# Routing of a mixture of experts in two steps, with the first five slots taken from the first six tiles

## The reference, cut to what matters

```python
x = x + cross_attention(layernorm(x), ctx)
x = x + self_attention(layernorm(x))
h = layernorm(x)                                   # (1024, 512)
logits = h @ gate_w.T + gate_b                     # (1024, 8)
topv, topi = top_k(logits, 2)
gate = softmax(logits where chosen, else -inf)     # two gates a row
out = x + sum over the 2 chosen experts e of gate[e] * (h @ expert_w[e] + expert_b[e])
```

## Time and profile before

| | |
|---|---|
| Time, median of 3 runs | 764.32 us (762.08 to 765.07) |
| Profiled execution | 759.4 us, span of the core 757.6 us |
| Granted TensorE clock, mean of the span | 0.99 |
| PE busy | 735.5 us, 97% |
| DVE, ACT, POOL busy | 554.2, 407.7, 350.3 us (73%, 54%, 46%) |
| DMA | 78.99 MB, mean 104 GB/s |

### The profile page before, as it was taken

The page is one execution under the profiler, slowest core; times in us unless marked ns, Lnnn a source line. Parts: engine busy times, 40 slices in busy tenths (PEclk is TensorE's granted clock), DMA queues, the critical chain, the costliest instruction groups (busy, mean ns, idle before and its releaser), DMA issues. The chain is left out here.

```text
span 757.6 us, 23202 instructions
## 1 busy us (share of the span) xinstructions
PE 735.5 (97%) x9488; PEld 644.7 (85%) x9489; DVE 554.2 (73%) x1293; ACT 407.7 (54%) x930; POOL 350.3 (46%) x364
## 2 busy tenths in 40 slices
PE   8999999999999999999999999999899999599997
PEld 7899989999899998999999999997677777578884
DVE  6768796967868768687696786877889998722236
ACT  5455666565566556655566555664566664033330
POOL 0664566456455644555545745541422221246630
PEclk9999999999999999999999999999999999789999
DMA  8410301221111011010110101141862229544538
GB/s 285 153 34 26 121 3 58 65 71 59 33 34 58 11 58 53 11 61 2 58 65 2 58 9 59 57 168 57 346 268 98 118 114 363 195 136 165 183 129 326
DMA packets 23317, 78.99 MB, mean 104 GB/s; under 512 B 3344, under 2 KB 4752, under 8 KB 20144
## 3 DMA queue, kind: packets, MB, share of 16 engines
q1 hardware_dynamic: 19536, 65.50, 24.0%
q0 software_dynamic: 3680, 12.06, 4.8%
HBM read 58.93 MB, written 18.61 MB: 102 GB/s over the span
## 5 line engine op out<-in xcount | busy, mean ns | idle before, releaser
L934 DVE TENSOR_TENSOR ctx_parts_lo<-craw,ctx_parts_hi 128x1032 fp32r<-128x1032 f32 (+1 forms) x56 | 66.5, 1188 | 3.6 <-ACT ctx_parts_hi L653 3.5
L1450 PE MATMUL bank<-ctx_parts_hi,wparts 128*128 128x258 f32 x224 | 67.2, 300 | 0.0
L1452 PE MATMUL bank<-ctx_parts_lo,wparts 128*128 128x258 f32 x224 | 63.5, 283 | 0.0
L1475 PE MATMUL bank<-wparts,ctx_parts_hi 128*128 128x256 f32 x224 | 63.3, 283 | 0.0
L1451 PE MATMUL bank<-ctx_parts_hi,wparts 128*128 128x258 f32 x224 | 63.2, 282 | 0.0
L1478 PE MATMUL bank<-wparts,ctx_parts_lo 128*128 128x256 f32 x224 | 63.1, 282 | 0.0
L1477 PE MATMUL bank<-wparts,ctx_parts_hi 128*128 128x256 f32 x224 | 62.9, 281 | 0.0
L684 ACT ACTIVATE v<-bank 128x512 f32<-128x512 f32 x56 | 33.3, 594 | 54.4 <-PE bank L1478 53.7
L496 POOL TENSOR_TENSOR k_trig<-kb_even,const 128x258 f32<-128x258 f32 (+1 forms) x42 | 49.0, 1167 | 28.8 <-ACT kb_even L674 28.1
L688 ACT ACTIVATE wraw<-wraw,nmax 128x257 f32<-128x257 f32 x96 | 47.8, 501 | 22.1 <-DVE nmax L1027 21.9
L1450 PE MATMUL bank<-ctx_parts_hi,w_sums_hi 128*128 128x258 f32 x168 | 52.7, 313 | 0.0
(11 more groups left out here) (418 smaller groups left out, 2588.4 us busy)
## 6 DMA issues: line engine op xcount, KB each, us to landing
craw<-ctx_t_dram SPq DMA_DIRECT2D x32, 516.0 KB, 4.3
expert_lo<-weights_dram SPq DMA_DIRECT2D x8, 1024.0 KB, 13.1
expert_hi_scratch<-wraw SPq DMA_DIRECT2D x16, 512.0 KB, 2.6
wparts<-expert_hi_scratch SPq DMA_DIRECT2D x8, 1024.0 KB, 9.1
wraw<-weights_dram SPq DMA_DIRECT2D x5, 1024.0 KB, 5.2
expert_lo<-ffn_out_scratch SPq DMA_DIRECT2D x16, 256.0 KB, 5.4
x<-x_dram SPq DMA_DIRECT2D x8, 256.0 KB, 4.4
late_weights_raw<-weights_dram SPq DMA_DIRECT2D x2, 1024.0 KB, 5.8
```

Source lines behind the costliest of these rows:

```text
L934: dve.tensor_tensor(dst[1], src, dst[0].bitcast(F32), ALU.subtract).then_inc(s_clo, 1)
L1450: pe.matmul(psum, whi_i[:, i, cols], hi[:, i, :], start=own and i == 0, stop=False, skip_group_check=not own)
L1452: last = pe.matmul(psum, whi_i[:, i, cols], lo[:, i, :], start=False, stop=i == 1, skip_group_check=not own)
L1475: pe.matmul(psum, hi[:, i, rows], whi_i[:, i, :], start=own and u == 0 and i == 0, stop=False, skip_group_check=True)
```

## The change

The routing is done in two steps.

- **First step.** `EARLY` grows from five tiles to six (tiles 0 to 5). `EK` = 12 is the number of their choices. Besides the ranks, PE counts the pairs of each expert in those six tiles (`early_count`). An expert's slots that are full from these six tiles alone can be known before tiles 6 and 7 are: DVE counts them (`full`), gives the first five of all such slots (`FIRST_SLOTS`) the numbers 0 to 4, and makes their table in one pass: `first_payload` holds 5 columns of row numbers and 5 of gates, `at_place` for the twelve early choices is made in two parts of six (`ONEHOT_PARTS`). PE multiplies it (12 blocks, 96 records) between the output projection of tile 7 and `x3_transposed(6)`. Then DVE writes `gather_row`, `scatter_row` and `slot_gate` of the five, and POOL issues the first four gathers.
- **POOL.** Both last `ffn_ln` (tiles 6 and 7) now stand behind these four gathers, and ahead of the gather of slot 4.
- **DVE.** The addition of tile 6's projection and the layer norm statistics of tile 6 move behind the first step; the early logits of tile 5 move ahead of it. Behind the statistics ten small instructions find the five slots' experts and correct ranks and counts for what the first five slots took.
- **PE.** The slots begin (transposes of slot 0) right behind the logits of tile 7. Then `late_ranks()`, the product of slots 0 and 1, and then `late_table()`: one table for the other 18 slots (`REST`), 16 blocks with 36 columns (row numbers and gates), 128 records. The transposes of the gates move from before the first product to between slots 3 and 4.
- **SP.** The loads of the last two experts (6 and 7) come ahead of the stores of `xn3` of tiles 6 and 7.
- Tensors move to other memory: the gathers' buffers into `craw`, `route_r` and `kept` into a new view at the place of `xn`.

The core of the diff:

```diff
-EARLY = TILES - 3
-ON_R = 10
-PAIRS = SLOTS + 1
+EARLY = TILES - 2
+FIRST_SLOTS = EARLY - 1
+REST = SLOTS - FIRST_SLOTS
+EK = 2 * EARLY
@@ gpsimd
-                ffn_ln(TILES - 2)
-                ffn_ln(TILES - 1)
...
                 pool.wait_ge(s_x3pad, 16)
-                pool.wait_ge(s_x3d, 16 * TILES)
+                pool.wait_ge(s_x3d, 16 * EARLY)
                 pool.wait_ge(s_rows, 1)
                 for i in range(AHEAD):
                     gather(i)
+                ffn_ln(TILES - 2)
+                ffn_ln(TILES - 1)
+                gather(AHEAD)
                 pool.wait_ge(s_rows, 2)
-                for i in range(SLOTS - LATE):
+                scatter(0)
+                scatter(1)
+                pool.wait_ge(s_x3d, 16 * TILES)
+                pool.wait_ge(s_rows, 3)
+                gather(FIRST_SLOTS)
+                pool.wait_ge(s_rows, 4)
+                for i in range(2, SLOTS - LATE):
@@ vector, behind place_in_tile(early_k)
+                dve.tensor_tensor(full_flags, early_count..., rc(R_TILE + 1, EARLY)..., ALU.is_ge)
+                dve.tensor_reduce(full, full_flags, AX.X, ALU.add)
                 dve.wait_ge(s_ohi, T + 2)
                 dve.tensor_tensor(otlo[:], ...)
-                ffn_ln_apply(T - 1)
+                (full_before, first_slot, picked, picked_sum, past_full, spot_open, spot, in_first: 8 instructions)
                 dve.wait_ge(s_sc, TILES)
-                for group in place_groups[:2]:
-                    place_onehots(*group)
+                for k0, k1 in ONEHOT_PARTS:
+                    dve.tensor_tensor(at_place[:, k0:k1, :], ...)
+                gates_of(0, EARLY, "")
+                (first_payload: 2 instructions)
                 dve.wait_ge(s_xpb, T + 1)
                 (x of tile 7 added in two halves)
+                dve.tensor_tensor(x[:, T - 1, :], b_cp, x[:, T - 1, :], ALU.add)
+                dve.wait_ge(s_table, 1)
+                (first_second, gather_row, scatter_row, slot_gate of the first five)
+                (statistics of tile 6, then of tile 7; ffn_ln_apply(T - 1); ten small instructions)
                 logits_evac(T - 1)
                 top(T - 1)
@@ tensor
-                pe.wait_ge(s_xo, T)
-                stay_awake(b_cp, 2)
+                pe.wait_ge(s_lg, T - 1)
+                stay_awake(b_x3, 2)
...
                     last.then_inc(s_cp, 1)
+                pe.wait_ge(s_payload, 1)
+                (first table)
                 x3_transposed(T - 1)
...
-                (late ranks, table of rows, table of gates)
+                pe.wait_ge(s_ewlo, HALVES)
+                slot_transposed(0, 0, 0)
+                late_ranks()
+                pe.wait_ge(s_lg, TILES)
+                pe.wait_ge(s_experts, 1)
+                pe.wait_ge(s_ehi, 16 * NE)
+                expert_step(0, 0, 0)
+                pe.wait_ge(s_xo, T + 2)
+                expert_step(1, 1, 0)
+                late_table()
+                for i in range(2, FIRST_SLOTS - 1):
+                    expert_step(i, i, 0)
+                gates_transposed()
```

More of the change, by code:

```diff
@@ L59 @@
 K2 = 2 * TILES
-EARLY = TILES - 3
-ON_R = 10
-PAIRS = SLOTS + 1
+EARLY = TILES - 2
+FIRST_SLOTS = EARLY - 1
+REST = SLOTS - FIRST_SLOTS
+EK = 2 * EARLY
+ROUTE_STEPS = (
+    "choice", "gap", "chosen", "gate_sum", "rank_parts", "rank", "tiles_up", "rank_tile", "place", "full_flags", "full",
+    "full_before", "first_slot", "picked", "picked_sum", "past_full", "spot_open", "spot", "in_first", "gate_den", "gate_0", "gate_1",
+    "first_second", "slot_end", "slot_past", "slot_expert", "slots_left", "slots_used", "used_tiles", "used_rows",
+    "used_mark", "rank_tile_left",
+    "centred", "late_choice", "late_gap", "late_chosen", "more", "late_rank_parts", "tiles", "late_rank", "upto", "late_tiles_up",
+    "start", "late_rank_tile", "start_of_choice", "late_place", "start_tile", "whole", "late_gate_den", "late_gate_0", "late_gate_1",
+    "in_tile", "second", "spare", "late_token", "begin", "past", "expert_f", "gates_by_choice", "late_in_tile")
+STEP = {name: n + 1 for n, name in enumerate(ROUTE_STEPS)}
 HALVES = 2 * NE
@@ L1762, in perceiver @@
[L1762 to L1768, removed]
+            kt_flat = kt[:].rearrange("p h k -> p (h k)")
+            carved = [wraw[0][:].rearrange("p c n -> p (c n)"), wraw[1][:].rearrange("p c n -> p (c n)"), kt_flat, xn[:], qkv[2]]
@@ new lines, in perceiver @@
+            gap, gexp, gden = (carve(TILES, at=BY_XN) for _ in range(3))
+            gtop = carve(TILES, 2, at=BY_XN)
+            gates = carve(TILES, S, at=0)
+            past = carve(REST, NE - 1, at=0)
+            expert_f = carve(SLOTS, at=0)
+            slot_gate = carve(SLOTS, at=0)
+            spare, second = carve(REST, at=0), carve(REST, at=0)
+            late_token = carve(LATE, at=0)
+            late_in_tile = carve(LATE, TILES, at=0)
+            begin = carve(NE, at=0)
+            full_flags = carve(NE, EARLY, at=BY_KT)
@@ L2105, in _ @@
                 last.then_inc(s_pbd, 1)
+                act.wait_ge(s_rt, STEP["gap"])
+                act.activation(gexp[:, 0:EARLY], gap[:, 0:EARLY], ACT.Exp).then_inc(s_gexp, 1)
                 act.wait_ge(s_av, T + 1)
@@ L2135, in _ @@
                 slot_hi(0, 0)
[L2136 to L2139, removed]
+                act.wait_ge(s_rt, STEP["late_gap"])
+                act.activation(gexp[:, EARLY:TILES], gap[:, EARLY:TILES], ACT.Exp).then_inc(s_gexp, 1)
+                act.wait_ge(s_rows, 2)
                 for i in range(SLOTS):
+                    if i == FIRST_SLOTS:
+                        act.wait_ge(s_rows, 4)
                     if i + 1 < SLOTS:
```

389 lines of the change are left out of this document (234 added, 155 removed).

## The result

The changed kernel takes 768.33 us (median of 16 runs, 764.66 to 769.54), the one before 764.14 us (16 runs beside it, 762.08 to 765.87): a ratio of 1.0053, interval 1.0041 to 1.0065, or +4.1 us. The difference is small, but the interval doesn't reach 1. The forecast was 767.5 us; the first rival said 769.1 us.

What follows compares the result with a forecast made beforehand. PE bounds the kernel, busy 97%; the change attacks 13.25 us from `kept_late` to the first product. +1.3 (second step's start) + 1.5 (late table) + 0.4 (gates' transposes) = +3.2 us, giving 767.5; 8-in-10 range 761.5 to 770.0.

Steps and rivals of the forecast that it cites:

- rival 1: Slower: clock at half through the whole first product (+1.1 us) and late table costing 2.0 us; 769.1 us, chance 0.28.
- The early part: PE's early ranks grow from 10 to 18 products (+0.90 us) and start 0.3 later; otlo on DVE comes 1.2 later.
- otlo to `gather_row`: DVE from otlo through small instructions, `at_place`, gates, payload and additions, then two instructions on the table: `gather_row` at 652.25.
- The hold: POOL's four gathers, 4.97 us, stand ahead of both `ffn_ln`; PE waits at `x3_transposed(6)` from 651.6 to 659.3.
- `kept_late` 6.05 behind 1/sqrt: Transposes of xn3 1.8 us at half clock, then 3.1 us from PE's logits of tile 6 to `kept_late`, at 664.25.
- first product 1.45 behind `kept_late`: Slot 0 is already transposed; late ranks and slot 1's transposes take 0.5 + 0.9 us, product 0 at 665.7.
- The first product's step: Slot 0's product, partly at half clock: 4.0 us taken, between bounds of 2.8 and 5.13; before it took 4.30.
- The late table: 128 records on PE between slots 1 and 2, at full clock without a wait: 1.1 to 2.0 us, taken 1.5.
- The transposes of gates: On PE, formerly under slot 0's wait, now costing 0.2 to 0.4 us, taken 0.4.
- Gather 5: Waits for the late table, out at 674.4, landed 679.3; PE wants it at 681, margin 1.7 us, so hidden.
- Rival 4: POOL reaches gather 5 2 us later, so PE stands a further 1 to 2 us in slot 4: 769, chance 0.05.
- Rivals 2 and 3: 2: layer norm not held by POOL's gathers, 762.8, chance 0.12. 3: also PE never loses its clock, 760.4, chance 0.08.

Runs made afterwards that it cites:

- first two traces of after: Two profiled executions of the changed kernel, unchanged, the second on another chip: 769.4 us and 764.36 us.
- third trace of after: The changed kernel again, unchanged, profiled on the third chip; its timed runs there took 768.3 us (6 runs), ratio 1.0064 to before.
- the reordered POOL: Changed kernel with POOL's order gather 0, 1/sqrt of tile 6, gather 1, 1/sqrt of tile 7, gathers 2 and 3: 763.82 us, ratio 1.0032 to before.

## Why the prediction was right, and where its terms were off

The order of events was right. The gathers leave 3.75 us earlier (18.60 to 14.85), POOL holds the layer norm behind them, PE stands idle in the place where the rows had been waited for, and every wait that was removed came back as another. The time lies in the range. It is 0.8 us above the forecast, 0.8 below rival 1, and the likeliest of the three cases (within 0.5%, 0.57) was missed by a hair: 1.0053. That the number is so near is luck in part. The traces of after add up to 8.1, 5.4 and 6.4 us behind t0 where the sum has 3.2, and the medians differ by 4.1. Term by term:

- *The early part, otlo at 6.25 after t0:* 7.29. I gave early ranks their 0.90, which they take, and left attention's product and the projection at their old speed. In the first two traces of after the clock is at 1.2 GHz for the product and nearly all of the projection: the product takes 1.94 in place of 1.08. In the third trace of after it takes 1.08 and otlo comes at 6.43, 0.2 from my figure. So the 0.85 between them is the clock's share, and whether it is paid changes from one execution to the next.
- *otlo to `gather_row`, 6.85:* 6.48. The first gather is 0.8 late: otlo's 1.04, less these 0.37, and 0.13 more from `gather_row` to POOL.
- *The hold, 4.97 us from first gather to 1/sqrt:* 4.98. The row of the gathers gave it exactly, and the reordered POOL confirmed it.
- *`kept_late` 6.05 behind 1/sqrt:* 6.20; *first product 1.45 behind `kept_late`:* 1.48. So its start, predicted as +1.6, is +2.57, and 0.8 of the 1.0 between them is the first gather's delay.
- *The first product's step, 4.0:* 4.87, between my 4.0 and the 5.13 of half clock throughout. Nine of the twelve products start at half clock, the first 0.57 and the others 0.43 to the next start. In these two traces this part of rival 1 came true nearly whole. The step of 2.89 with PE kept busy shows it is the clock. In the third trace of after the step is 3.82, close to my 4.0.
- *The late table, 1.5:* 1.60 in the unbroken form, with the next step 0.5 longer, which I had not counted; 2.66 where PE pauses inside it, with 0.70 on the next. Rival 1's 2.0 lies between.
- *The transposes of gates, 0.4:* 0.20.
- *Gather 5, due 36.5 us after t0:* 39.54, since two of the steps ahead of it are longer. Landed 3.6 later, it is still 2.5 ahead of slot 5's transposes at 45.66. Rival 4 didn't happen.
- *Rivals 2 and 3* (layer norm not held): refuted, as the hold is there to 0.01 us.
- *No slot after the fifth other than 3.24 us:* this sign of being wrong did appear, as the slot of 4.62 us in the first and third trace of after. Nothing in the prediction has it.
- *The edges of the clock in before:* the granted share of a stretch is a mean of 1.0 and 0.5, so 0.79 puts the fall at 653.6 and 0.89 the rise at 667.2, not 653.8 and 667.1. No term rests on it.
- *The tail unchanged:* right for after (18.2 us from the column sums to the end in both traces, 18.4 in before). It doesn't hold for the six variants with idle products in the gap, where DVE waits 0.59 to 1.67 us for `expert_lo`.

Put right, the sum is 3.2 + 1.0 (otlo) + 0.9 (first product) + 0.1 + 0.5 (table and the step behind it) - 0.2 = 5.5, which is the second trace's 5.4. The third trace comes to +1.96 for the start and -0.48 for the first product's step, near my +1.6 and -0.3, and then +4.9 for the table, its pauses, the gates and the late slot: +6.4. So with the clock held early the sum fails only from the table on, by the pauses, the slow step behind them and the late slot. The medians give +4.1, and +4.4 on the third chip. That the traces' steps from t0 are more than the medians' stays open: traces of before with pauses of their own would explain it, but the two taken show none.

The Trainium skill, "TensorE: Matmul & The Clock Gate", section "Wait — 56ns, not 53.3ns?", has no start to start under about 25 ns. By that the late table would be an estimated 3.2 us; 128 records in 1.58 us are 12.3 ns each. Counted by products, of two records each, they are 24.7 ns, which would fit. But the 16 products (32 records) of 8 columns of one tile's logits start 0.27 us before the next set (639.76 and 640.03 in after), 17 ns each. So by either count the measurement decides against it for products that take turns on four column groups.

What stays open: why the variant with thirteen idle products in the gap (beyond the 1.3 us at its end) and the one with none ahead of attention show a gain in their traces and none in the medians; which semaphore ACT stands for in the late slot; and whether PE's pauses are instructions that have not come in time. The packets of the instruction queue lie with most of the pauses, but no run moved a packet and left the rest, so this is a coincidence in time and not a cause shown.

## What to carry to other kernels

When work is brought forward on an in-order engine, list what it is moved past: here four gathers of 1.25 us each were put ahead of two instructions of 0.6 us that the critical path needed, and interleaving them was worth 3.3 us of start. Read the granted clock at the new place of each product and not at its old one, since a change in order also changes where PE has rested. Trace the same code more than once before a difference of a microsecond is explained: the clock's early fall and the pauses come in some executions and not in others. And price a run of narrow products by more than its rate. Putting full products between two halves of the table took its pauses away, but a run of only 32 records had them elsewhere in the same trace.

## What the runs showed of the chip that I had not expected

- PE pauses inside straight runs of narrow products with nothing to wait for: 0.43 and 0.45 us around the 121st record of 128, 1.83 us after the 195th of 256, and 0.45 to 0.50 three times inside 32 records. From execution to execution they stand at nearly the same records (the first behind 120 to 122 of the table, and behind 11 or 12 of the logits). The other single tables of 128, and both halves of 64, show none.
- Once regained in the gap, the clock could be lost again: with six idle products it was back at 658 and at half by 664, with thirteen it stayed at 1.00 through PE's waits, and the first product's step was 2.89 us against 4.44.
- The clock's early fall isn't fixed by the code. With both idle products ahead of attention, the product of 32 records took 1.93 or 1.94 us in five traces and 1.08 in two. With none it took 1.08 in three and 1.31 in one, and with the pair split around the early ranks 1.29.
- The same kernel differs by 3 us between chips (before: 761 and 764), and its first 65 us by 1.8 to 2.0 us between executions of one kernel (3.4 over all fourteen traces).
